# Large copies of a four-layer graph network cut into 112 and 13 partitions, and waited for at their use

## The reference

```python
x = layernorm(x + L0(x, adj, h0, y))        # 0.9 * normalised (adj * (y @ y.T)) @ x + 0.1 * h0
x = layernorm(x + L1(x, adj, W1, W2, W3, U1, U2, ln_g, ln_b))
x = layernorm(x + L2(x, adj, W, a_l, a_r, bias))   # graph attention of 4 heads
x = layernorm(x + L3(x, adj, ...))                 # graph attention, then a GRU cell

# L1, two steps: R = row-normalised (adj + I), A = top-p attention on Xa
for n in range(2):
    A  = top_p_attention(Xa)
    Xf = R @ Xf
    Xa = A @ Xa
    Z  = Z + Xf @ U1[n].T + Xa @ U2[n].T
h = X + Z          # then a layer norm with gain ln_g and bias ln_b
```

## Time and profile before

| | |
|---|---|
| median of three executions | 7123.94 us (7119.68 to 7130.17) |
| the profiled execution | 7131.35 us |
| its span in the profile | 7129.6 us |
| TensorE busy | 4537.1 us, 64% of the span |
| VectorE busy | 5314.4 us, 75% |
| ScalarE busy | 2161.8 us, 30% |
| mean of the DMA traffic | 77 GB/s |
| mean granted TensorE clock | 0.828 |

### The profile page before, as it was taken

One profiled execution on the slowest core, in us unless ns is written; L12 is line 12 of the kernel. 1 busy time (PEld: TensorE's weight loads), 2 busy tenths in 40 slices (PEclk: granted clock), 3 DMA queues, 4 the chain that ended last, 5 costly groups with the idle time before them and its releaser, 6 DMA issues. The chain is left out here.

```text
span 7129.6 us, 80171 instructions
## 1 busy us (share of the span) xinstructions
PE 4537.1 (64%) x27812; PEld 3255.7 (46%) x27812; DVE 5314.4 (75%) x13021; ACT 2161.8 (30%) x3033; POOL 344.0 (5%) x170
## 2 busy tenths in 40 slices
PE   5995688888665364523475588553337888835981
PEld 2442467676554354522464477453311222205981
DVE  4885577777448888887888899886349999974864
ACT  2332565656311011100132244222132222213541
POOL 0000000000110000000000000010000222020000
PEclk9997788888897787866787799786669999977995
DMA  5551000000032122111111122110103333303840
GB/s 171 202 199 57 1 2 1 1 1 1 21 132 97 57 86 85 75 40 43 58 66 57 50 87 93 59 58 17 29 16 130 107 110 109 110 26 144 292 161 29
DMA packets 192671, 549.28 MB, mean 77 GB/s; under 512 B 20027, under 2 KB 77126, under 8 KB 192126
## 3 DMA queue, kind: packets, MB, share of 16 engines
q1 hardware_dynamic: 187069, 539.58, 21.2%
q0 software_dynamic: 5120, 3.97, 0.2%
HBM read 526.73 MB, written 16.68 MB: 76 GB/s over the span
## 5 line engine op out<-in xcount | busy, mean ns | idle before, releaser
L655 PE MATMUL ps<-ident,arena 125*125 125x125 f32 x3200 | 562.9, 311 | 1161.4 <-DVEq L1139 1161.4
L655 PEld LDWEIGHTS ps<-ident,arena 125*125 125x125 f32 x3200 | 492.9, 224 | 1201.7 <-DVEq L1139 1201.7
L687 PE MATMUL ps<-arena 125*125 125x129 f32 x6400 | 834.5, 289 | 308.9 <-DMA arena<-in_adj_tiles 301.1
L663 PE MATMUL ps<-arena,turned 125*125 125x129 f32 x6400 | 943.7, 297 | 104.7 <-ACT turned L759 104.7
L1438 DVE SCALAR_TENSOR_TENSOR arena<-arena,pair 125x1000 f32<-125x1000 f32 x800 | 939.3, 1253 | 71.3 <-ACT arena L1401 71.3
L759 ACT ACTIVATE turned<-ps 125x500 f32<-125x500 f32 x800 | 464.4, 587 | 1699.4 <-PE ps L655 1698.2
L687 PEld LDWEIGHTS ps<-arena 125*125 125x125 f32 x6400 | 782.5, 199 | 380.6 <-DMA arena<-in_adj_tiles 298.1
L663 PEld LDWEIGHTS ps<-arena,turned 125*125 125x125 f32 x6400 | 869.3, 208 | 121.3 <-ACT turned L759 117.6
L1456 PE MATMUL ps<-arena 125*64 125x500 f32 x3200 | 765.0, 601 | 192.9 <-DVE arena L1438 192.8
L1092 DVE SCALAR_TENSOR_TENSOR arena<-arena,wt 125x5000 f32<-125x5000 f32 x80 | 434.1, 5427 | 194.6 <-issue 194.6
L1456 PEld LDWEIGHTS ps<-arena 125*64 125x64 f32 x3200 | 197.9, 137 | 756.9 <-DVE arena L1438 525.1
(11 more groups left out here) (343 smaller groups left out, 6073.1 us busy)
## 6 DMA issues: line engine op xcount, KB each, us to landing
arena<-in_adj_wide SPq DMA_DIRECT2D x400, 500.0 KB, 4.5
arena<-in_adj_tiles SPq DMA_DIRECT2D x400, 488.3 KB
arena<-in_adj_wide SPq DMA_DIRECT2D x100, 1000.0 KB, 4.8
x_saved<-arena SPq DMA_DIRECT2D x4, 2500.0 KB
arena<-x_saved SPq DMA_DIRECT2D x3, 2500.0 KB
arena<-att_saved SPq DMA_DIRECT2D x1, 2519.5 KB
arena<-in_x SPq DMA_DIRECT2D x1, 2500.0 KB
arena<-in_h SPq DMA_DIRECT2D x1, 2500.0 KB
```

What stands on the lines that cost most here:

```text
L655: mm = pe.transpose(banks_turn[:, g % 2, c * P:(c + 1) * P], work[b % DEPTH][:, j:j + P], ident[0:P, 0:P])
L663: mm = pe.matmul(acc_attend, turned[:, g % 2, c * P:(c + 1) * P], nodes(v_attend, FA)[:, j, :], start=(j == 0), stop=(j == NB - 1))
L687: mm = pe.matmul(acc_spread, ring[:, j * P:(j + 1) * P], values[:, j, :], start=(j == 0), stop=False)
```

## The change

Each copy of a whole node array is issued as two, partitions 0 to 111 and 112 to 124. Each has a semaphore of its own for its purpose, which lives through the whole program, and is waited for by the engine or queue that needs the data. The load of h0 comes last in the first block. The load of `att_saved` is issued in the first `transposed` stage of the middle of layer 1, one load of `x_saved` in the second; `mix_in` reads VC and writes VB, so that the second load of `x_saved` is not there. In layer 2 the load into X2 is issued at the start of the elementwise block. The stores of `x_saved` after layers 2 and 3 are dropped, and `out` is stored from `finish_layer("l3f")`.

```diff
+        def load_by_parts(sp, dst, src, semaphore):
+            for lo, hi in ((0, 112), (112, P)):
+                sp.dma_start(dst[lo:hi], src[lo:hi]).then_inc(semaphore, 16)
...
-                sp.dma_start(nodes(VA, FA)[:, :, 0:F], nat(x)).then_inc(s_x, 16)
-                sp.dma_start(nodes(VC, FA)[:, :, 0:F], nat(h0)).then_inc(s_x, 16)
+                load_by_parts(sp, nodes(VA, FA)[:, :, 0:F], nat(x), s_x)
...
+                load_by_parts(sp, nodes(VC, FA)[:, :, 0:F], nat(h0), s_h0)
                 sp.wait_ge(s_x, 208)
...
                     sp.wait_ge(s_done, 1)
-                    sp.dma_start(nat(x_saved), y).then_inc(s_out, 16)
-                    sp.wait_ge(s_out, 16)
+                    if goes_to is x_saved:
+                        load_by_parts(sp, nat(x_saved), y, s_saved)
+                    elif goes_to is out:
+                        load_by_parts(sp, nat(goes_to), y, s_stored)
+                        sp.wait_ge(s_stored, 32)
...
             agg, x0, h = (nodes(at, FA)[:, :, 0:F] for at in (VB, VA, VC))
+            v.wait_ge(s_h0, 32)
...
-            copy_stage("l1o", [(nodes(VD, FA), att_saved.rearrange("(b p) f -> p b f", p=P))])
-            normalise(VD, VA)
-            transposed(VC, FA, KT)
-            transposed(VB, FA, XT)
+            transposed(VC, FA, KT, lambda sp: load_by_parts(
+                sp, nodes(VD, FA), att_saved.rearrange("(b p) f -> p b f", p=P), s_attended))
+            transposed(VB, FA, XT, lambda sp: load_by_parts(sp, nodes(VC, FA)[:, :, 0:F], nat(x_saved), s_restored))
+            normalise(VA)
             transposed(VA, FA, EB)
+            normalise(VD, loaded=s_attended)
             transposed(VD, FA, EB + N)
-            copy_stage("l1b", [(nodes(VB, FA)[:, :, 0:F], nat(x_saved)), (nodes(VC, FA)[:, :, 0:F], nat(x_saved))])
-            mix_in("l1m", VB, [(KT, 192), (XT, 448), (EB, 192 + F), (EB + N, 448 + F)])
+            mix_in("l1m", VB, VC, [(KT, 192), (XT, 448), (EB, 192 + F), (EB + N, 448 + F)])
...
                     sp.wait_ge(s_w, 64)
+                    sp.wait_ge(s_saved, 64)
...
-            copy_stage("l2b", [(nodes(ERB + 2 * NB * F, F), nat(x_saved))])
...
+                @block.sync
+                def _(sp):
+                    load_by_parts(sp, nodes(X2, F), nat(x_saved), s_restored)
...
+                    v.wait_ge(s_restored, 64)
                     v.tensor_tensor(nodes(VA, FA)[:, :, 0:F], y, nodes(X2, F), ALU.add)
...
-            finish_layer("l2f", lambda v: None, Y, VA)
+            finish_layer("l2f", lambda v: None, Y, VA, None)
...
-            finish_layer("l3f", lambda v: None, T3, VA)
-
-        copy_stage("end", [(nat(out), nodes(VA, FA)[:, :, 0:F])])
+            finish_layer("l3f", lambda v: None, T3, VA, out)
```

More of the change, by code:

```diff
@@ L85, in gnn_kernel @@
         ps = ctx.enter_context(nc.psum_tensor("ps", [128, 8, 512], F32))
+        def load_by_parts(sp, dst, src, semaphore):
+            for lo, hi in ((0, 112), (112, P)):
+                sp.dma_start(dst[lo:hi], src[lo:hi]).then_inc(semaphore, 16)
+        s_h0, s_saved, s_restored, s_attended, s_stored = (ctx.enter_context(nc.semaphore("x_" + n)) for n in (
+            "h0", "saved", "restored", "attended", "stored"))
         def rows(at, width, parts=P):
@@ L301, in _, with finish_layer @@
                      .then_inc(s_copied, 1)
-        def finish_layer(name, prepare, scratch_at, target):
+        def finish_layer(name, prepare, scratch_at, target, goes_to):
             with nc.semaphore(name + "_var") as s_var, nc.semaphore(name + "_std") as s_std, \
-                    nc.semaphore(name + "_done") as s_done, nc.semaphore(name + "_out") as s_out, \
+                    nc.semaphore(name + "_done") as s_done, \
                     nc.Block() as block:
@@ L345, in residual0, with transposed @@
             v.drain()
-        finish_layer("l0", residual0, VD, VA)
-        def transposed(src, width, dst):
+        finish_layer("l0", residual0, VD, VA, x_saved)
+        def transposed(src, width, dst, meanwhile=None):
             past = banks["used"]
@@ L353, in transposed @@
             with nc.Block() as block:
+                if meanwhile:
+                    @block.sync
+                    def _(sp):
+                        meanwhile(sp)
                 @block.tensor
@@ L595, in chosen_rows @@
                           .then_inc(chosen_in[b % DEPTH], 16)
+                    if not arranged:
+                        sp.wait_ge(s_saved, 32)
                     if spreads:
@@ L1181, in _, with mix_in @@
                     nc.switch_bb(name + "_over")
-        def mix_in(name, h_at, terms):
+        def mix_in(name, out_at, h_at, terms):
             with nc.semaphore(name + "_m") as s_m, nc.semaphore(name + "_a") as s_a, nc.Block() as block:
@@ L1200, in _ @@
                 def _(v):
+                    v.wait_ge(s_restored, 32)
                     for g in range(NG):
                         v.wait_ge(s_m, g + 1)
-                        hs = nodes(h_at, FA)[:, g * GC:(g + 1) * GC, 0:F]
-                        v.tensor_tensor(hs, hs, ps[0:P, g % 2, :].rearrange("p (c f) -> p c f", c=GC),
+                        hs, sums = (nodes(at, FA)[:, g * GC:(g + 1) * GC, 0:F] for at in (h_at, out_at))
+                        v.tensor_tensor(sums, hs, ps[0:P, g % 2, :].rearrange("p (c f) -> p c f", c=GC),
                                         ALU.add).then_inc(s_a, 1)
@@ L1219, in _, with normalise @@
                     sp.wait_ge(s_c, 16 * len(pairs))
-        def normalise(*ats):
+        def normalise(at, loaded=None):
             def body(v):
[L1224 to L1233, removed]
+                if loaded is not None:
+                    v.wait_ge(loaded, 32)
+                r = recip[:, 0:NB]
+                v.tensor_copy(r.unsqueeze(2), nodes(at, FA)[:, :, F:FA])
+                v.drain()
+                v.reciprocal(r, r)
+                v.drain()
+                t = nodes(at, FA)[:, :, 0:F]
+                v.tensor_tensor(t, t, per_row(r), ALU.mult)
+                v.memset(nodes(at, FA)[:, :, F:FA], 1.0)
+                v.drain()
             vector_stage(body)
@@ L1269, in gnn_kernel @@
                 nodes(VA, FA)[:, :, 0:F], nodes(VB, FA)[:, :, 0:F], nodes(VC, FA)[:, :, 0:F], ALU.add),
-                v.drain()), VD, VA)
+                v.drain()), VD, VA, x_saved)
         def shift_terms(name, heads, width, values):
```

## The result

| | median | executions |
|---|---|---|
| before | 7123.26 us | 7119.68 to 7130.17, 4 |
| changed | 6905.28 us | 6903.05 to 6907.43, 4 |

The ratio is 0.9693, with a 95% interval of 0.9676 to 0.971: 218 us, or 3.1%, less. The forecast was 6878 with a range of 6850 to 6928. The way and the main mechanism were right, and the time is 27 us above the forecast.

The account below looks back on a forecast made before the run. Eleven node-array copies waited for in the open, some 275 us, were taken to bound it; savings of 38 + 17.5 + 84 + 17.5 + 26 + 25 + 41 = 249 us gave 6878 us, range 6850 to 6928.

Parts of the forecast that it names:

- What bounds it: Whole program: eleven 2.5 MB copies waited for with no engine computing, about 25 us each, some 275 of 7129.6 us.
- The price of a copy in two parts: Every node-array copy: 112 partitions 7.0 us plus 13 partitions 1.0, together 8.0 us for 24.9.
- My bound with the slower rate: Copies at 215 GB/s: 3.7 us more at six places, 2 in the middle's first stage, 24 us, giving 6902.
- Start: Before the first VectorE multiplication: about 41 us for 79.2, taken as -38, bounds -35.6 to -43.6.
- the 21.55: At the start, microseconds from w1T being taken to the end of the wait, assumed to stay unchanged.
- Stores: After layers 0 and 1: SP held 7.0 us by the second part, 8.0 us for 25.5, -17.5 each.
- Rival C: SP is not held by the second part; both stores gain 7 more, the middle 1: 6863 us, chance 0.14.
- Middle: Middle of layer 1, up to mix_in: 127.6 us become 45.5, -82; a faster first mix_in group makes it -84.
- A: All split copies: two parts no faster than one copy; gains sum to 131 us, time 6997, chance 0.05.
- B: Part of 13 partitions runs on one engine, 12.9 us and not 1.0: +48, 6926 us, chance 0.07.
- D: Step s0: lower granted TensorE clock; eating 249 us needs a fall from 0.82 to 0.65; chance 0.01.
- the signs that I named for a wrong prediction: VectorE waiting at L345, L1247, L1224 or L1767, or unchanged stages between the copies running at another clock.

Follow-up runs that it names:

- dropped_only: The kernel before without the two late stores of x_saved and the second load in layer 1: 7047.44 us against 7125.21, ratio 0.989.
- h0_last: The changed kernel with h0 loaded behind the last adjacency piece of layer 0: 6890.12 us, ratio 0.9666.
- the h0 kernels: Two versions of the changed kernel, h0 loaded after the 21st adjacency piece of layer 0 (6895.86 us) or behind the last (6890.12 us).
- second_next: The changed kernel with only the first part of two x_saved stores issued in finish_layer, the second in the next block: 6889.07 us, ratio 0.9666.
- The copies by themselves: Kernels without the network, SP only copying node arrays one after the other: 125 partitions 28.6 us as a load, 112 and 13 together 15.6.
- combined: The changed kernel with h0_last and second_next together, and one part of a load for each block in the middle of layer 1: 6871.93 us, ratio 0.9639.

## Why the prediction was right, and where it was off

**What bounds it** was right. Eleven waits in the open were the cost; dropped_only returned 78 us for three, and no computing time moved.

**The price of a copy in two parts** is the term that was mis-sized: 8.0 us, measured 15.6 as a load and 12.8 as a store. I took the time that an issue was held behind one copy of 125 partitions, 24.9, for the time of that copy, and scaled it by rows. Alone that copy takes 28.6 us as a load, and the first part 12.6 where 7.0 were priced. The hold was right (7.7), the landing is another thing, and only where the data is waited for does it count. That is why the sum was off by 28 and not by 11 times 6: stores after layers 0 and 1 (17.2 and 17.6 for 17.5) and the load in layer 2 never waited for a landing. My bound with the slower rate, 6902, is close to the measured 6905 by luck: it adds 3.7 us at each of six places, the two stores among them, which came out as forecast, while the start and the middle lost more.

**Start**, 38 forecast, 22.6 measured. That h0 stands ahead of the adjacency was counted, at 8 us less 3 that it would fill. It cost 15 (h0_last), 10 more than counted; the h0 kernels show that it is h0's place, and not which of its parts. In the change the traffic between 28 and 36 us, with h0 and yT under way, was 83 and then 55 GB/s; why two loads side by side are so slow stays open. The other 5 us are the 21.55 that I let stand between w1T and the end of the wait: in h0_last, without h0, they are 26.6 (10.24 to 36.82). The rest of x, which alone takes 15.6 us, still lands in them, and with its second part on another queue the first multiplication came 3.9 us earlier.

**Stores.** SP held by a second part, and the barrier with it: 8.3 and 7.8 us for 8.0, and second_next confirms the cause. Rival C, no hold, is refuted by the same run.

**Middle**, 82 forecast, 72.3 measured. The second stage was to take 8.4 us and took 15.1. Its first issue was taken after 1.1 us, as forecast; its second was held for 13.47 and not for 7.0. The copies by themselves show the same hold without a network: behind 112 and 13 partitions the second part of the next array was held for 13.05 (second row), and with three parts of 112 and none of 13 the third was held for 10.52 (third row) where the second had been held for 7.41:

```profile
4929.26 13.47 SPq L90 DMA_DIRECT2D arena<-x_saved  x1
...
279.88 13.05 SPq L116 DMA_DIRECT2D arena<-in_h  x1
...
308.77 10.52 SPq L116 DMA_DIRECT2D arena<-in_h  x1
```

So a hold of 7 us is that behind a copy that finds the queue empty. Behind a queue with work in it I should have taken about 10.5, and some 2.5 to 3 more for the 13 partitions; while these ran, the traffic was 82 to 88 GB/s for three microseconds (4931 to 4934). combined, without a second issue in any block, won 7.9 there. Most of the other 2.4 us goes with the clock: each half of `normalise` now leaves TensorE idle for 7 us and more, and the transposes behind the second run slowly (40 in 7.93 us, 198 ns each, where 8 took 1.04 in the earlier trace rows, 130 ns). The granted clock was 0.83 in the stage behind the first half and 0.71 behind the second, where the last three transpose stages of before had 1.00; they took 8.3 and 8.9 us for 7.3.

**The rivals.** A, no faster in parts: refuted by the copies alone, 15.6 for 28.6. The 6934 of the moves without the split is no measure of its 6997: rival A has a second issue that holds SP for 22 us, and there is none in that kernel. B, 13 partitions on one engine: refuted, 5.0 us and not 13. D: the clock did not fall; the mean was 0.828 before and is 0.837, and in step `s0` it is 0.82 in both. Of the signs that I named for a wrong prediction none came: no wait at L345, L1247, L1224 or L1767 was for a load.

**The Trainium skill.** The count of engines by the page "DMA: Bandwidth & Descriptors", section "Why a DMA increments its semaphore by 16 and not by 1", agrees with the ratio of the two shares: 0.36 is 0.31 of 1.18, and 5 is 0.31 of 16. My reading of 0.36 as 5.8 busy engines was wrong, since the same reading makes 18.9 engines of 1.18. That section says nothing of how long a row takes, and that grew. An estimate by its count of engines: 98 GB/s on 5 are 26 ns for each row of 512 bytes, 228 on 16 are 36 ns. The advice in "SBUF — State Buffer", "Summary: rules for kernel authors", one DMA and not several, is given for 128 partitions. For 125 it does not hold: two took 15.6 us and one 28.6.

## What to carry to other kernels

Look first for stretches in which no engine computes, and remove the copy or the wait before making the copy faster: here the moves alone gave 193 of 218 us. A second large copy behind a first holds its issuing queue, and through a barrier every engine; issue one for each block, or the last of a run where nothing waits for the queue. Price a copy by a run of it alone from issue to landing, and not by the time that it blocks the next issue; and price a hold by what is already in the queue, 7.4 us behind the first of three parts and 10.5 behind the second.

## What the hardware showed beyond that

A split that looks better on paper is not: 120 and 5 partitions took 20.3 us as a load and 18.7 as a store, 112 and 13 took 15.6 and 12.8; 120 partitions alone took 17.4 for 7% more data than the 12.6 of 112. Nothing here says why.

A load of 16 partitions took 5.0 us, and one of 5 partitions with a third of the bytes 4.8. Either the price of such a small copy is nearly all fixed, or it goes by the rows of one partition, 40 in both; no copy here tells the two apart.

The small part can go first. In the copies by themselves 13 partitions and then 112 took 16.0 us (120.95 to 136.94), about as long as the other way round, but the second issue was taken after 0.44 us and not 7.36. No kernel here tries that order at a place where the hold counts.
